# Layer-3 self-attention of a four-layer decoder: bank plan of the spread products, place of the output products, place of the exponential table load

## The chip, the cores and the metric

The kernel runs on one core of one Trainium2 chip (trn2). The metric is the time of one execution on the device in microseconds, as the median over several runs. The kernel before takes 3958.56 us (three runs, 3958.35 to 3964.81).

## What is computed

The program computes twelve sublayers, four layers of self-attention, cross-attention and a feed-forward part, each added to the residual `x` (4 batches x 512 tokens x 256 features, all in float32). The change touches one of them alone, the self-attention of layer 3. It attends over the axis of length 4 (called s for the query and t for the key), separately for each of the 512 tokens and 16 heads of 16 features, with a learned vector for each distance s - t added to keys and values:

```python
Q = (x @ w_q.T).reshape(seq_len, batch, N_HEADS, D_K)   # seq_len = 4, batch = 512
K = (x @ w_k.T).reshape(seq_len, batch, N_HEADS, D_K)
V = (x @ w_v.T).reshape(seq_len, batch, N_HEADS, D_K)
rk = rel_k[rel_idx]
rv = rel_v[rel_idx]
scores = jnp.einsum('sbhd,tbhd->sbth', Q, K) * scale
scores = scores + jnp.einsum('sbhd,std->sbth', Q, rk) * scale
attn = jax.nn.softmax(scores, axis=-1)
out = jnp.einsum('sbth,tbhd->sbhd', attn, V)
out = out + jnp.einsum('sbth,std->sbhd', attn, rv)
out = out.reshape(seq_len, batch, D_MODEL)
return out @ w_o.T + b_o
```

The softmax runs over the last axis, which holds the 16 heads.

## The kernel before

The work of each engine is written out by hand, one instruction stream for each, and ordered by semaphores. Each sublayer is a stage of its own, and all engines meet between stages, so nothing of the next stage starts before the last instruction of this one. The stage is `l3_attn`. It runs in these steps.

1. TensorE (function `unit`, L3900 to L3916) turns the normed tokens and makes queries, keys and values, feature by token, in banks 4 to 7 of PSUM. ScalarE moves each out (`move`, L4007). VectorE multiplies queries with keys for each of the 16 pairs (s, t) (`multiply`, L4068), and TensorE sums them over the heads' features (`scores`, L3922) into banks 0 to 3.
2. Softmax, for t = 0 to 3: ScalarE copies the scores out of PSUM (L4013), TensorE turns them (L3929), VectorE takes maximum and difference (`below_max`, L4104, L4106), ScalarE the exponential (L4016), VectorE sum, reciprocal and share (`share`, L4111 to L4115), TensorE turns the shares back (`turn_shares`, L3935) and ScalarE copies them to `shares_T` (L4019). Ahead of the first exponential the compiler puts an ACT_TABLE_LOAD (L4016).
3. Spread and weigh: `items` lists the 16 pairs as (sp, t, i), with s = 2 sp + i. Two items that differ only in i make a couple. `spread_two` (L3938 to L3953) makes one couple: a product with a constant 32-row matrix copies the 16 shares of a token to its 256 features, two chunks of 128 features for each item, so four products and four banks for a couple. The two items use different 32-row strips. VectorE then makes `(value + rel_v) * spread share` out of PSUM (`weigh`, L4078), 128x1024 for one item, into a ring of eight buffers `weighted_values`. GpSimd (POOL) adds items n and n + 2 of a group of four (L4041), giving eight `attended_pairs_T`.
4. Outputs: `outputs(s)` (L3955 to L3967) multiplies the pairs with `w_o` in 16 products of 128x256, two banks for each s; VectorE adds each half to the residual (`add`, L4083 to L4087).

In steps 3 and 4 the order is given by three things. The spread products use BANKS = 3 slots of two banks, banks 0 to 5, and item n takes slot n % 3. `spread_two` waits, before its first product, until both slots of its couple are free:

```python
for n in (first, first + 1):
    if n >= BANKS:
        pe.wait_ge(weighted, n - BANKS + 1)
    else:
        pe.wait_ge(shares_moved, S)
        pe.wait_ge(unit_moved, len(units))
```

The outputs use banks 6 and 7, whatever s is, and wait for the addition of the s before (`added`). And the streams interleave: TensorE makes `outputs(0)` between couples 5 and 6 (counted from 0), `outputs(1)` between couples 6 and 7, `outputs(2)` and `outputs(3)` at the end; VectorE does the additions of s = 0 after item 13 and those of s = 1 after item 15.

Of the kernel before, what the change touches and what calls it, by code (L numbers as in the profile page):

```python
# [16 lines left out]
ALU = mybir.AluOpType  # L17
ACT = mybir.ActivationFunctionType
AX = mybir.AxisListType

P = 128
D = 256
KC = D // P
B = 4
# [3808 lines left out]
def l3_attn(k):  # L3833
# [10 lines left out]


    nc = k.nc
    S, RING, BANKS = B, 8, 3
    pairs = [(s, t) for n in range(S) for s, t in
             [(m, n) for m in range(n)] + [(n, m) for m in range(n)] + [(n, n)]]
    units = [(kind, s, c) for s in range(S) for kind in ("turn", "query", "key") for c in range(KC)] + [  # L3850
# [2 lines left out]
    ps = k.ps  # L3853
    with ExitStack() as st:
# [3 lines left out]
        head_spread = k.const("head_spread", st)  # L3858
# [12 lines left out]
        e = k.sb("shares_T", [P, S, T], st)  # L3871
        av = k.sb("weighted_values", [P, RING, KC, T], st)
        o = k.sb("attended_pairs_T", [P, 8, KC, T], st)
        items = [(sp, t, i) for sp in range(2) for t in range(S) for i in range(2)]


        def real(w, t):

            return w[:, t, :].rearrange("p (g h) -> p g h", h=32)[:, :, 0:16]

        with signals(nc, "loaded", "stats", "aggr", "shift", "rstd", "normed", "unit_made", "unit_moved",
# [7 lines left out]
            @block.sync  # L3889
            def _(sp):  # L3890
                for w in (wq, wk, wv, rk, rv, head_rows, head_spread, wo, *k.stage_rows):
                    whole = tuple(slice(None) for _ in w.src.shape)
                    sp.dma_start(w.dst[whole], w.src[whole]).then_inc(loaded, 16)
# [4 lines left out]
            def _(pe):  # L3898
# [39 lines left out]
                def spread_two(sp, t):  # L3938
                    first = 8 * sp + 2 * t
                    pe.wait_ge(shares_moved, t + 1)  # L3940
                    for n in (first, first + 1):
                        if n >= BANKS:
                            pe.wait_ge(weighted, n - BANKS + 1)
                        else:
                            pe.wait_ge(shares_moved, S)
                            pe.wait_ge(unit_moved, len(units))
                    for c in range(KC):
                        for i in range(2):
                            r = slice(32 * (2 * sp + i), 32 * (2 * sp + i) + 32)
                            last = pe.matmul(ps[:, 2 * ((first + i) % BANKS) + c, :], head_spread[r, c, :], e[r, t, :],  # L3950
                                             start=True, stop=True)
                            if c == KC - 1:
                                last.then_inc(spread, 1)  # L3953

                def outputs(s):  # L3955
                    sp, i = s // 2, s % 2
                    pe.wait_ge(summed, 4 * sp + 2 + i + 1)
                    for h in range(2):
                        if s:
                            pe.wait_ge(added, 2 * (s - 1) + h + 1)  # L3960
                        for t in (2 * h, 2 * h + 1):
                            for j in range(2):
                                for c in range(KC):
                                    last = pe.matmul(ps[:, 6 + h, t % 2 * D:(t % 2 + 1) * D],
                                                     o[:, 4 * sp + 2 * j + i, c, t * P:(t + 1) * P], wo[:, c, :],
                                                     start=j == 0 and c == 0, stop=j == 1 and c == KC - 1)
                        last.then_inc(made, 1)  # L3967
# [4 lines left out]
                n = 0  # L3972
# [18 lines left out]
                    turn_shares(t)  # L3991
                for sp in range(2):
                    for t in range(S):
                        if sp and t >= 2:
                            outputs(t - 2)
                        spread_two(sp, t)
                outputs(2)
                outputs(3)

            @block.scalar  # L4000
            def _(act):
                dst = {"turn": xT, "query": qT, "key": kT, "value": vT}

                def move(u):
                    kind, s, c = units[u]
                    act.wait_ge(unit_made, u + 1)
                    act.copy(dst[kind][:, s, c, :], ps[:, 4 + u % 4, :]).then_inc(unit_moved, 1)  # L4007

                for u in range(len(units)):
                    move(u)  # L4010
                act.wait_ge(scored, len(pairs))
                for t in range(S):
                    act.copy(sc[:, t, :], ps[:, t, :]).then_inc(scores_moved, 1)  # L4013
                for t in range(S):
                    act.wait_ge(below, t + 1)
                    act.activation(real(er, t), real(er, t), ACT.Exp, scale=0.25).then_inc(exped, 1)  # L4016
                for t in range(S):
                    act.wait_ge(shares_turned, t + 1)
                    act.copy(e[:, t, :], ps[:, t, :]).then_inc(shares_moved, 1)  # L4019
# [25 lines left out]
            def _(dve):  # L4045
# [26 lines left out]
                def weigh(n):  # L4072
                    sp, t, i = items[n]
                    s = 2 * sp + i
                    dve.wait_ge(spread, n + 1)
                    if n >= RING:
                        dve.wait_ge(summed, 2 * ((n - RING) // 4) + i + 1)
                    dve.scalar_tensor_tensor(out=av[:, n % RING, :, :], in0=vT[:, t, :, :],  # L4078
                                             scalar=rv[:, s - t + S - 1:s - t + S],
                                             in1=ps[:, 2 * (n % BANKS):2 * (n % BANKS) + 2, :], op0=ALU.add,  # L4080
                                             op1=ALU.mult).then_inc(weighted, 1)

                def add(s, h):  # L4083
                    dve.wait_ge(made, 2 * s + h + 1)
                    dve.wait_ge(biased, 2 * s + h + 1)
                    rows = k.x[:, TT * s + 2 * h:TT * s + 2 * h + 2, :].rearrange("p t d -> p (t d)")
                    dve.tensor_tensor(rows, rows, ps[:, 6 + h, :], ALU.add).then_inc(added, 1)  # L4087

                batch_stats(0)
                batch_stats(1)  # L4090
# [31 lines left out]
                        share(t - 1)  # L4122
                for n in range(16):
                    weigh(n)
                    if n == 13:
                        add(0, 0)
                        add(0, 1)
                    if n == 15:
                        add(1, 0)
                        add(1, 1)  # L4130
                for s in (2, 3):
                    for h in range(2):
                        add(s, h)
                dve.wait_ge(added, 2 * S)
# [814 lines left out]
```

## Time and profile before

| | |
|---|---|
| median of three runs | 3958.56 us (3958.35 to 3964.81) |
| the profiled execution, its own time | 3928.34 us |
| its span, from first to last instruction | 3926.0 us |
| busy over the whole span: PE, DVE, ACT, POOL | 89%, 56%, 38%, 35% |
| mean granted TensorE clock over the span | 0.931 of full speed |
| stage `l3_attn`, first to last DVE instruction | 2975.59 to 3144.63 us of the span |

A profile is one execution. Its times count from the first instruction. PE is the matmul part of TensorE, PEld its weight loads, DVE is VectorE, ACT ScalarE, POOL GpSimd, SP the engine that issues DMAs. A float32 matmul stands in the profile as two records, so the four products of a couple are eight. In a row of the timeline the first number is the start, the second the length, and the bracket holds how long the engine had been idle and what ended that. A row of busy time by stretch has from and to, the length, the busy time of PE, PEld, DVE, ACT and POOL with the number of instructions of each, the granted clock, and the share and GB/s of DMA. "Granted clock" is the share of TensorE's 2.4 GHz that it was given: 1.00 or, at the lower of the two levels, 0.50 (1.2 GHz).

### The profile page before, as it was taken

Reading aid. Unit: us, or ns where it says so; the run is one execution under the profiler, and the core shown is the slowest. Engines: PE = TensorE matmul, PEld = TensorE weight load, DVE = VectorE, ACT = ScalarE, POOL = GpSimd, SP = SyncE. Lnnn points to the kernel's source line nnn. Section 1 sums busy time; section 2 is a strip of 40 time slices with the busy share of each in tenths; the row PEclk is TensorE's granted clock in tenths of the full one; section 3 lists DMA queues with packets and bytes.
Section 4 is the critical chain, followed back from the end, with each engine's and each line's share of the span. In section 5 each row is a group of like instructions: output and inputs, shape, how many; then the busy total and the mean of one; then the engine's idle time right before and its main releaser. Section 6 shows DMA issues by size and latency. Waiting matters only on the chain. (4 is left out here: it accounts for less than half of the span.)

```text
span 3926.0 us, 54458 instructions
## 1 busy us (share of the span) xinstructions
PE 3483.6 (89%) x18930; PEld 2234.7 (57%) x18930; DVE 2189.6 (56%) x5367; ACT 1495.9 (38%) x3039; POOL 1371.7 (35%) x1904
## 2 busy tenths in 40 slices
PE   7998897899999977789798999998996779996997
PEld 5675684445555567344444555555893445554896
DVE  5374444646556567666366676765334356665454
ACT  2253112434434364233244444443451144442553
POOL 2141441423223245233254444533422144442311
PEclk9999978999999988899799999999898789997998
DMA  2004001000000000000100000001321000003212
GB/s 101 1 1 124 14 1 46 1 1 1 1 1 1 13 1 8 17 1 1 49 1 1 1 1 1 1 1 50 135 76 52 0 29 1 1 1 160 72 60 84
DMA packets 48718, 108.85 MB, mean 28 GB/s; under 512 B 6660, under 2 KB 32900, under 8 KB 46404
## 3 DMA queue, kind: packets, MB, share of 16 engines
q1 hardware_dynamic: 40964, 84.88, 6.4%
q0 software_dynamic: 7488, 20.49, 1.5%
q8 instruction: 158, 2.59, 0.3%
q14 instruction: 108, 0.88, 0.1%
HBM read 70.67 MB, written 34.68 MB: 27 GB/s over the span
## 5 line engine op out<-in xcount | busy, mean ns | idle before, releaser
L2653 POOL TENSOR_SCALAR probs<-probs,inv_sum 128x512 f32<-128x512 f32 x640 | 438.2, 698 | 1007.1 <-DVE inv_sum L2774 1006.8
L2616 ACT ACTIVATE probs<-psum_banks,neg_max 128x576 f32<-128x576 f32 x640 | 468.6, 737 | 743.3 <-DVE neg_max L2857 743.3
L2857 DVE TENSOR_REDUCE neg_max<-psum_banks 128x1 f32<-128x576 f32 x640 | 454.7, 752 | 213.5 <-PE psum_banks L2491 206.9
L2491 PE MATMUL psum_banks<-keys_T,queries_T 64*128 64x288 f32 x2560 | 406.8, 437 | 52.5 <-ACT probs L2616 43.2
L2783 DVE COPY probs_T<-psum_banks 128x512 f32<-128x512 f32 x640 | 408.7, 679 | 4.0 <-PE psum_banks L2411 4.0
L2491 PEld LDWEIGHTS psum_banks<-keys_T,queries_T 64*128 64x128 f32 x2560 | 224.8, 189 | 269.6 <-ACT probs L2616 148.4
L2411 PE MATMUL psum_banks<-ident,probs 128*128 128x128 f32 x2560 | 357.4, 283 | 3.2 <-POOL probs L2653 2.3
L2411 PEld LDWEIGHTS psum_banks<-ident,probs 128*128 128x128 f32 x2560 | 281.2, 143 | 128.9 <-POOL probs L2653 64.8
L2441 PE MATMUL psum_banks<-probs_T,values 128*64 128x512 f32 x1280 | 309.3, 605 | 2.2 <-issue 2.2
L4406 PE MATMUL psum_banks<-sorted_T,tile_weights 128*128 128x128 f32 x2208 | 266.2, 278 | 4.9 <-ACT tile_weights L4496 4.9
L4406 PEld LDWEIGHTS psum_banks<-sorted_T,tile_weights 128*128 128x128 f32 x2208 | 258.5, 195 | 5.7 <-issue 5.6
L2853 DVE TENSOR_TENSOR psum_banks<-psum_banks,key_mask 128x128 f32<-128x128 f32 x192 | 57.4, 299 | 279.9 <-PE psum_banks L2491 279.9
L2665 POOL TENSOR_TENSOR square_sum<-square_sum,neg_half 128x8 f32<-128x8 f32 x102 | 167.1, 1640 | 68.9 <-DVE square_sum L2749 67.6
L4309 POOL DMA_INDIRECT expert_outputs<-expert_rows,output_index x92 | 89.6, 974 | 268.8 <-DVE expert_rows L4683 122.1
L4422 PE MATMUL psum_banks<-w_L_experts_down,hidden_T 128*128 x736 | 177.2, 384 | 7.0 <-DVE expert_rows L4683 3.6
L2346 PE MATMUL psum_banks<-w_L_xattn_Wkv,batch_normed_T 128*128 128x512 f32 x320 | 157.7, 617 | 0.0
L2441 PEld LDWEIGHTS psum_banks<-probs_T,values 128*64 128x64 f32 x1280 | 78.5, 136 | 132.3 <-issue 121.7
L4422 PEld LDWEIGHTS psum_banks<-w_L_experts_down,hidden_T 128*128 128x128 f32 x736 | 134.4, 193 | 23.0 <-issue 8.2
L4496 ACT COPY tile_weights<-w_L_experts_up 128x1024 f32 (+1 forms) x92 | 135.3, 1472 | 25.3 <-issue 25.3
L1962 ACT ACTIVATE probs_T<-psum_banks 128x512 f32<-128x512 f32 (+3 forms) x128 | 83.0, 701 | 127.4 <-PE psum_banks L1899 126.5
L2656 POOL TENSOR_TENSOR context_probs<-probs,inv_sum 128x128 f32<-128x128 f32 x320 | 128.6, 402 | 0.0
L2616 ACT ACTIVATION_READ_ACCUMULATOR probs<-psum_banks,neg_max 128x1 f32 x640 | 125.4, 196 | 0.0
(534 smaller groups left out, 6119.2 us busy)
## 6 DMA issues: line engine op xcount, KB each, us to landing
normed<-sorted_rows SPq DMA_DIRECT2D x30, 385.5 KB, 3.3
sorted_rows<-zero_rows SPq DMA_DIRECT2D x8, 1028.0 KB, 14.6
w_L_experts_down<-in_L_experts_down SPq DMA_DIRECT2D x2, 4096.0 KB, 31.2
normed<-expert_outputs SPq DMA_DIRECT2D x8, 1024.0 KB, 6.9
w_L_xattn_Wkv<-in_L_xattn_Wkv SPq DMA_DIRECT2D x2, 2048.0 KB, 8.1
w_L_experts_up<-in_L_experts_up SPq DMA_DIRECT2D x1, 4096.0 KB, 12.9
sorted_rows<-zero_rows SPq DMA_DIRECT2D x4, 899.5 KB, 14.5
x_res<-in_x SPq DMA_DIRECT2D x4, 512.0 KB, 7.0
```

Of the source, the lines that this page charges most:

```text
L2346: last = pe.matmul(k.ps[:, 7, :], rows, wkv[:, c, W + a * 512:W + (a + 1) * 512], start=c == 0, stop=c == KC - 1)
L2411: last = pe.transpose(k.ps[:, 4 + n % 2, c * P:(c + 1) * P], prob[:, (b * NS + s) % PB, at + c * P:at + (c + 1) * P], k.ident[:, :])
L2441: last = pe.matmul(k.ps[r, 6, :], values[:, b % VB, c, (2 * j + h) * 64:(2 * j + h + 1) * 64], pT[:, q % 2, h, c, :], start=c == 0, stop=F ...
L2491: last = pe.matmul(k.ps[:, 2 * h + a, 0:HALF], qT[r, b % 2, j, t * P:(t + 1) * P], kT[r, j, k0:k0 + HALF], start=True, stop=True)
L2616: act.activation(prob[:, g % PB, h * w:(h + 1) * w].rearrange("p (a n) -> p a n", a=2), k.ps[:, 2 * h:2 * h + 2, 0:HALF], ACT.Exp, bias=nm ...
L2653: pool.tensor_scalar(w, w, inv[:, g % 4, h:h + 1], 1.0, ALU.mult, ALU.mult).then_inc(shared, 1)
L2665: pool.tensor_tensor(ss[:, i % 4, 2, :], ss[:, i % 4, 1, :], k.half[:, 0:8], ALU.pow).then_inc(inverted, 1)
L2783: dve.tensor_copy(pT[:, q % 2, h, :, t * P:(t + 1) * P], k.ps[:, 4 + n % 2, :].rearrange("p (c q) -> p c q", q=P)).then_inc(copied, 1)
L2857: dve.tensor_reduce(nmax[:, g % 4, h:h + 1], k.ps[:, 2 * h:2 * h + 2, 0:HALF], AX.XY, ALU.max, negate=True).then_inc(maxed, 1)
L4406: last = pe.matmul(ps[:, 2 * (n % 2) + part, f * P:(f + 1) * P], wt[:, n % 2, c, part * 512 + f * P:part * 512 + (f + 1) * P], xsT[:, n % ...
L4422: last = pe.matmul(ps[:, 6, 0:D], h[:, n % 2, f * P:(f + 1) * P], w_down[:, f // F, f % F * D:f % F * D + (E - 1) * STEP + D][:, bass.ds(a ...
L4496: act.copy(wt[:, n % 2, :, :], w_up[:, :, 0:(E - 1) * STEP + UP][:, :, bass.ds(at, UP)]).then_inc(weights_copied, 1)
```

## The change

`BANKS` becomes 4, so that the spread products take all eight banks; item n takes slot (n + 2) % 4, so items 0 and 1 begin in banks 4 to 7, which the softmax doesn't use. Only items 2 and 3 wait for all four shares to be moved. All outputs come after all couples, each in the two banks of `item_bank(s)`, and wait for the weighing of the item that last used them instead of for additions; VectorE adds them all after its last item. A one-column exponential (`exp_seed`) stands at the head of ScalarE's stream.

```diff
-    S, RING, BANKS = B, 8, 3
+    S, RING, BANKS = B, 8, 4
...
+        seed = k.sb("exp_seed", [P, 1], st)
         items = [(sp, t, i) for sp in range(2) for t in range(S) for i in range(2)]
 
+
+        def item_bank(n):
+
+            return 2 * ((n + 2) % BANKS)
...
                     for n in (first, first + 1):
                         if n >= BANKS:
                             pe.wait_ge(weighted, n - BANKS + 1)
+                        elif n >= 2:
+                            pe.wait_ge(shares_moved, S)
                         else:
-                            pe.wait_ge(shares_moved, S)
                             pe.wait_ge(unit_moved, len(units))
...
-                            last = pe.matmul(ps[:, 2 * ((first + i) % BANKS) + c, :], head_spread[r, c, :], e[r, t, :],
+                            last = pe.matmul(ps[:, item_bank(first + i) + c, :], head_spread[r, c, :], e[r, t, :],
...
                 def outputs(s):
                     sp, i = s // 2, s % 2
                     pe.wait_ge(summed, 4 * sp + 2 + i + 1)
+                    pe.wait_ge(weighted, len(items) - BANKS + s + 1)
                     for h in range(2):
-                        if s:
-                            pe.wait_ge(added, 2 * (s - 1) + h + 1)
...
-                                    last = pe.matmul(ps[:, 6 + h, t % 2 * D:(t % 2 + 1) * D],
+                                    last = pe.matmul(ps[:, item_bank(s) + h, t % 2 * D:(t % 2 + 1) * D],
...
                 for sp in range(2):
                     for t in range(S):
-                        if sp and t >= 2:
-                            outputs(t - 2)
                         spread_two(sp, t)
-                outputs(2)
-                outputs(3)
+                for s in range(S):
+                    outputs(s)
...
+                act.activation(seed[:, :], k.half[:, 0:1], ACT.Exp)
                 for u in range(len(units)):
                     move(u)
...
                 for n in range(16):
                     weigh(n)
-                    if n == 13:
-                        add(0, 0)
-                        add(0, 1)
-                    if n == 15:
-                        add(1, 0)
-                        add(1, 1)
-                for s in (2, 3):
+                for s in range(S):
                     for h in range(2):
                         add(s, h)
```

TensorE's stream at the end of the stage, before. `head_spread` products are the couples (four for each), `w_o` products the outputs (16 for each s):

```order
L3914 MATMUL psum_banks<-normed_T,w_L_attn_w_v 128x512 x4
L3929 MATMUL psum_banks<-ident,scores_T 128x128 x16
L3935 MATMUL psum_banks<-ident,exps 128x128 x16
L3950 MATMUL psum_banks<-shares_T,w_head_spread 128x512 x24
L3964 MATMUL psum_banks<-w_L_attn_w_o,attended_pairs_T 128x256 x16
L3950 MATMUL psum_banks<-shares_T,w_head_spread 128x512 x4
L3964 MATMUL psum_banks<-w_L_attn_w_o,attended_pairs_T 128x256 x16
L3950 MATMUL psum_banks<-shares_T,w_head_spread 128x512 x4
L3964 MATMUL psum_banks<-w_L_attn_w_o,attended_pairs_T 128x256 x32
```

The same place after the change:

```order
L3927 MATMUL psum_banks<-products,w_head_rows 32x512 x2
L3919 MATMUL psum_banks<-normed_T,w_L_attn_w_v 128x512 x4
L3934 MATMUL psum_banks<-ident,scores_T 128x128 x16
L3940 MATMUL psum_banks<-ident,exps 128x128 x16
L3956 MATMUL psum_banks<-shares_T,w_head_spread 128x512 x32
L3969 MATMUL psum_banks<-w_L_attn_w_o,attended_pairs_T 128x256 x64
```

The number of products is the same, 32 and 64; the 32 products of the outputs of s = 0 and 1 have moved behind the last couple.

ScalarE's stream at the softmax, before:

```order
L4007 COPY values_T<-psum_banks 128x512 x8
L4013 COPY scores_T<-psum_banks 128x512 x4
L4016 ACT_TABLE_LOAD
L4016 ACTIVATE exps<-exps 128x16x16 x4
L4019 COPY shares_T<-psum_banks 128x512 x4
```

ScalarE's stream at the head of the stage, after the change:

```order
L4003 UNCONDITIONAL_BRANCH
L4012 ACT_TABLE_LOAD
L4012 ACTIVATE exp_seed<-neg_half 128x1
L4010 COPY normed_T<-psum_banks 128x512 x2
L4010 COPY queries_T<-psum_banks 128x512 x2
```

The one table load of the stage has moved from between the score copies and the exponentials to the stage's head, with the one-column exponential behind it; no other table load has come or gone in the program.

## Rows read from the trace of the kernel before

**Rows 1.** The page's first line: the span of the profiled execution.

```profile
span 3926.0 us, 54458 instructions
```

**Rows 2.** Timeline of PE from the last turned shares to the stage's end.

```profile
3065.83 2.19 PE L3935 MATMUL psum_banks<-ident,exps 128*128 128x128 f32 x8 [0.75 <-DVE exps L4115]
3068.90 3.78 PE L3950 MATMUL psum_banks<-shares_T,w_head_spread 32*128 32x512 f32 x8 [0.88 <-ACT shares_T L4019]
3074.12 3.78 PE L3950 MATMUL psum_banks<-shares_T,w_head_spread 32*128 32x512 f32 x8 [1.43 <-DVE weighted_values L4078]
...
3094.97 3.78 PE L3950 MATMUL psum_banks<-shares_T,w_head_spread 32*128 32x512 f32 x8 [1.43 <-DVE weighted_values L4078]
3098.68 9.86 PE L3964 MATMUL psum_banks<-w_L_attn_w_o,attended_pairs_T 128*128 128x256 f32 x32
3108.47 1.99 PE L3950 MATMUL psum_banks<-shares_T,w_head_spread 32*128 32x512 f32 x8
3113.70 8.83 PE L3964 MATMUL psum_banks<-w_L_attn_w_o,attended_pairs_T 128*128 128x256 f32 x32 [3.25 <-DVE x_res L4087]
...
3128.25 15.65 PE L3964 MATMUL psum_banks<-w_L_attn_w_o,attended_pairs_T 128*128 128x256 f32 x64 [3.80 <-POOL attended_pairs_T L4041]
```

**Rows 3.** Timeline of DVE: weighing (L4078), additions (L4087), first instruction of the next stage.

```profile
3072.69 2.47 DVE L4078 SCALAR_TENSOR_TENSOR weighted_values<-values_T,w_rel_v_columns,psum_banks 128x1024 f32<-128x1024 f32 x2 [5.83 <-PE psum_banks L3950]
...
3110.49 2.47 DVE L4078 SCALAR_TENSOR_TENSOR weighted_values<-values_T,w_rel_v_columns,psum_banks 128x1024 f32<-128x1024 f32 x2 [9.26 <-PE psum_banks L3950]
...
3143.94 0.69 DVE L4087 TENSOR_TENSOR x_res<-x_res,psum_banks 128x512 f32<-128x512 f32 x1 [2.77 <-PE psum_banks L3964]
3145.67 0.43 DVE L2712 BATCH_NORM_STATS2 batch_stat<-x_res 128x6 f32<-128x256 f32 x1 [1.04 <-PEq L45]
```

**Rows 4.** Busy time and granted clock by stretch of this stage.

```profile
3063.20:3098.70 35.50, 25.95 (x61) 9.76 (x61) 15.80 (x20) 2.64 (x6) 9.30 (x4) 0.50 0.00 0
3098.70:3104.20 5.50, 5.50 (x15) 4.42 (x14) 2.47 (x2) 0.00 (x0) 4.08 (x2) 0.50 0.00 0
...
3128.20:3131.40 3.20, 3.15 (x8) 2.50 (x9) 0.00 (x0) 0.00 (x0) 2.29 (x1) 0.50 0.03 5
3131.50:3144.00 12.50, 12.40 (x58) 10.58 (x56) 2.12 (x4) 0.00 (x0) 0.00 (x0) 1.00 0.00 0
```

**Rows 5.** ACT: its first copy of the stage, and the softmax.

```profile
2981.59 0.59 ACT L4007 COPY normed_T<-psum_banks 128x512 f32<-128x512 f32 x1 [31.73 <-PE psum_banks L3908]
...
3059.14 1.28 ACT L4016 ACT_TABLE_LOAD   x1
...
3068.06 0.59 ACT L4019 COPY shares_T<-psum_banks 128x512 f32<-128x512 f32 x1 [0.49 <-PE psum_banks L3935]
```

**Rows 6.** Timeline of DVE: the stage's first instruction, and the softmax.

```profile
2975.59 1.41 DVE L4049 BATCH_NORM_STATS2 token_stat<-x_res 128x6 f32<-128x256 f32 x4 [1.46 <-PEq L45]
...
3059.72 0.42 DVE L4106 TENSOR_TENSOR exps<-psum_banks,highest 128x256 f32<-128x256 f32 x1
3060.89 0.42 DVE L4111 TENSOR_REDUCE sums<-exps 128x16 f32<-128x256 f32 x1 [0.75 <-ACT exps L4016]
```

**Rows 7.** Instructions on the tile `weighted_values`: ns min/median/max.

```profile
L4078 DVE SCALAR_TENSOR_TENSOR weighted_values<-values_T,w_rel_v_columns,psum_banks x16: 1272/1278/1282, 3072.7 to 3125.7; 128x1024 f32<-128x1024 f32 x16
L4041 POOL TENSOR_TENSOR attended_pairs_T<-weighted_values x8: 2338/2348/2357, 3079.3 to 3128.2; 128x1024 f32<-128x1024 f32 x8
```

**Rows 8.** Busy time and granted clock in the self-attention stage of layer 2.

```profile
1645.00:1655.00 10.00, 8.00 (x82) 3.90 (x84) 6.51 (x11) 3.66 (x7) 3.19 (x10) 1.00 0.01 2
```

**Rows 9.** Groups by line on PE there, 1625 to 1665: a product of 32 rows.

```profile
L1886 PE MATMUL psum_banks<-keys_T,queries_T 32*128 32x512 f32 x16 | 2.3, 640 | 0.0
```

**Rows 10.** Timeline of POOL: the additions of the bias (L4035).

```profile
2988.32 7.45 POOL L4035 TENSOR_TENSOR x_res<-x_res,row_vectors 128x512 f32<-128x512 f32 x6
2996.64 3.47 POOL L4035 TENSOR_TENSOR x_res<-x_res,row_vectors 128x512 f32<-128x512 f32 x2 [0.87 <-DVE normed L4060]
```

**Rows 11.** Timeline of DVE beside the second of these rows.

```profile
2996.48 1.27 DVE L4068 SCALAR_TENSOR_TENSOR products<-keys_T,w_rel_k_columns,queries_T 128x1024 f32<-128x1024 f32 x1
```

More of the change, by code:

```diff
@@ L4079, in weigh @@
                                              scalar=rv[:, s - t + S - 1:s - t + S],
-                                             in1=ps[:, 2 * (n % BANKS):2 * (n % BANKS) + 2, :], op0=ALU.add,
+                                             in1=ps[:, item_bank(n):item_bank(n) + 2, :], op0=ALU.add,
                                              op1=ALU.mult).then_inc(weighted, 1)
@@ L4086, in add @@
                     rows = k.x[:, TT * s + 2 * h:TT * s + 2 * h + 2, :].rearrange("p t d -> p (t d)")
-                    dve.tensor_tensor(rows, rows, ps[:, 6 + h, :], ALU.add).then_inc(added, 1)
+                    dve.tensor_tensor(rows, rows, ps[:, item_bank(s) + h, :], ALU.add).then_inc(added, 1)
                 batch_stats(0)
```

## The prediction

> **What bounds the kernel now.** The chain of waits that ended last covers only the tail of the program, so I read the stage itself: the timeline of PE, then that of DVE beside it, then busy time with the granted clock by stretch. Since all engines meet between stages, whatever this stage saves comes off the program.
>
> In the timeline of PE the reader is to see a rhythm: a couple of spread products takes 3.78 us, then PE stands 1.43 us for a weighing, and the next couple starts 5.22 us after the first [rows 2]. The DVE timeline has the other half: weighing starts 3.79 us after the couple (3068.90 to 3072.69) and takes 2.47 us for two items [rows 2, 3]. Neither engine is full: with three slots a couple needs a slot that the couple before still holds, until its first item is weighed, so the period is 3.79 of PE, one item of 1.28, and the rest a signal, some 0.15. This holds for couples 0 to 5 (3068.90 to 3098.68). After them PE makes the outputs of s = 0 in 9.86 us while DVE idles 9.26 us, couple 6 in 1.99 us, and then waits 3.25 us for the first addition; the same happens again, with couple 7 and another wait of 3.80 us for POOL's sums [rows 2, 3]. The last addition starts at 3143.94 and takes 0.69, the next stage's first instruction follows at 3145.67 [rows 3].
>
> The third view explains the 3.78 against the 1.99: the granted clock is 0.50 through the first six couples, though PE is 73% busy there (25.95 of 35.50), and becomes 1.00 only 5.5 us into the gapless outputs. At 3128.2 outputs begin at 0.50 again and run at 1.00 after 3.2 us [rows 4].
>
> I count from the start of couple 0 (3068.90) to the end of the last addition (3144.63): **75.73 us before**.
>
> **The change, part by part.**
>
> 1. *Four slots.* Couple k now waits for couple k - 2 only. At the low clock PE is the longer one: eight records in two concurrent strips last 3.71 us from one start to the next where no wait lies between (3094.97 to 3098.68 [rows 2]); I estimate 3.4 between two couples, twice the 1.7 that the full clock gives (1.99 less the same tail of 0.3). DVE's 2.47 fits beneath. At the full clock it turns round: PE 1.99, DVE 2.47. A slot pair then needs PE's 2.02 to the first weighing (3108.47 to 3110.49), 2.47 of DVE and 0.15 of signal, 4.64 us for two couples, or 2.32 each, under 2.47: DVE sets the pace [rows 2, 3].
>
> 2. *Which clock.* The trace of before never shows couples without gaps, so I bound it: all eight at the low level, or the rise a few us after the start. Gapless work was granted the full clock after 3.2 us in one row, and after 9.2 us in the other if the couple before the outputs counts (3094.97 to 3104.2) [rows 2, 4]. Now PE has no gap from the turned shares onwards: couple 1 needs no weighing, and couple 2 waits for items 0 and 1, done at 3.79 + 2.47 + 0.15 = 6.4 us, when couple 1 ends (6.8). I take the rise in the middle, about 5 us after the start. Then DVE starts at 3.79 and is not starved again. Does the clock stay up with PE pausing 0.5 us in every 2.47, 80% busy by the profile's measure? Layer 2's self-attention, which has products of 32 rows too, ran at 1.00 with PE busy 8.00 of 10 us [rows 8, 9]. So I say yes.
>
> 3. *The spread phase then.* DVE begins at 3.79; couple 7 waits for six couples weighed: 3.79 + 6 x 2.47 + 0.15 = 18.8. It takes 1.99, so outputs may begin at 20.8. Their new wait, item 12 weighed, ends at 3.79 + 14.8 + 1.28 = 19.9, earlier. Behind that wait on PE's queue lie only the outputs, and their waits on POOL are met early: the sums for s = 0 and 1 are made while DVE weighs, the last one two sums of 2.35 after item 14, at 3.79 + 15 x 1.24 + 4.7 = 27 [rows 7], before outputs of s = 3 want it at 41.5. POOL needs 4.7 for two sums per 4.94 of DVE, so the ring of eight doesn't hold DVE either.
>
> 4. *All outputs at the end.* 64 products, 128 records. At the full clock one half of an s takes the 2.77 idle and 0.69 busy that separate two additions, 3.46 us [rows 3]; eight of them 27.6. Before, the same products took 9.86 + 8.83 + 15.65 = 34.3 [rows 2], partly at the low clock. Additions move behind all weighings on DVE; that costs nothing, since each bank is used once and nobody waits. Only the last shows: some 0.25 for the tail of the last product and 0.69. Sum: 20.8 + 27.6 + 0.9 = **49.3 us**, against 75.7: 26.4 saved.
>
> 5. *An earlier couple 0.* It needs one share moved and banks 4 to 7, not all four shares. Before it stood behind the last copy (3068.06 + 0.59) and began at 3068.90; the turned shares end at 3068.02 [rows 2, 5]. Saved 0.9. Couple 1 waits for all four copies, done 3.4 us before it wants them.
>
> 6. *Table load.* It took 1.28 us between score copies and exponentials, and ended at 3060.42 [rows 5]. DVE waited 0.75 for the exponential between 3059.72 and 3060.89; that goes, then DVE's own chain is next [rows 6]. Saved 0.75 at most; the load now runs from about 2975.6, where ACT has idled and has no work until 2981.59 [rows 5, 6]. A load of 1.28 and a one-column exponential, which I bound by a copy of 512 columns, 0.59, lie in these 6 us. Without that cover they would cost 1.3 to 1.9. I take 0.7.
>
> No DMA or POOL instruction moves, and the next stage begins as before. Together 26.4 + 0.9 + 0.7 = **28.0 us**. The sum is against the profiled execution: 3928.34 would become 3900.3. The median stands 30 us above that execution; its span is 3926.0 [rows 1]. I take the 30 us as common to both kernels, so 3958.56 - 28.0 = **3930.6 us**, 0.7% less.
>
> **Rivals.**
>
> *A. The couples stay at the low clock.* For it: six couples at 73% busy never got the full clock [rows 4]. The Trainium skill has a rule that speaks against this change ("TensorE: Matmul & The Clock Gate", section "A second HAM failure mode: psum-queue depth-cycling"): cycling through PSUM banks, with small pauses between groups of matmuls, made the clock swing between its two levels. By that rule the stage of layer 2 should have swung as well, and it held 1.00 [rows 8]; in this stage the low clock with its pauses agrees [rows 4]. As a mechanism here: couples follow at 3.4, couple 7 begins at 23.9, outputs at 27.6, and their first 5.5 us are at half speed, 2.7 lost: 27.6 + 27.6 + 2.7 + 0.9 = 58.8, saved 16.9 + 1.6 = 18.5, **3940 us**. Against it: the pauses of 1.43 are gone [rows 2].
>
> *B. POOL and DVE block each other.* DVE now weighs without pause while POOL sums. Such a block exists: six bias additions took 1.24 each, but two beside a DVE product took 3.47 [rows 10, 11]. The Trainium skill ("SBUF — State Buffer", "Who interferes with whom") gives the case: a DVE instruction with two inputs in SBUF against a GpSimd one that reads SBUF. By it the weighing, with one array in SBUF and one in PSUM, is free of it. The rows say the same: the sums took 2338 to 2357 ns, whether a weighing lay beside them, as at 3079.3, or not [rows 7]. If all ran in series, item 12 would be weighed at 3.79 + 13 x 1.24 + 6 x 2.35 = 34.0 and outputs would begin there, not at 20.8: 13.2 less saved, **3944 us**.
>
> *C. Slower: the sums become the bound.* Same place, larger price. All outputs of s = 2 and 3 wait for a chain of eight sums that begins 7.5 us in. With x us for each, the end is 7.5 + 8x + 6.9 + 0.9. That reaches the 77.3 of before (75.7 + 1.6) at x = 7.8, and at 9 it is 10 us slower, **3968 us**. The sum measures 2.35 in all eight cases [rows 7], so x would have to grow more than threefold. Nothing in the trace hints at it.
>
> *D. The change doesn't do it:* another wait keeps the 5.2 us rhythm. The stream shows none. Gain then only from outputs and start, some 5 us, **3953**.
>
> **How the numbers follow.** Forecast 0.75, A 0.18, B 0.03, C 0.02, D 0.02. A measurement of this kernel can tell about 0.2%, 8 us, from no change; forecast, A and B lie beyond it: faster 0.96, D is same 0.02, C slower 0.02. The range: the clock's rise anywhere from 3 to 9 us moves the forecast by 1 to 2, other moments of rising and falling in the 780 us behind the stage by some 4 (the runs of before spread over 6.5). That gives 3924 to 3937 for the forecast alone, and A asks for 3943 above. I give 3922 to 3943.
>
> **What would show it.** In the profile after: couple starts 3.4 us apart at first, then 2.5; DVE's weighings in one row with at most one or two waits of a us; granted clock 1.00 within 10 us of couple 0 and kept; additions 3.46 apart; the last addition some 49 us behind couple 0; no wait of PE on additions. Part 6 is right if the first sum of exponentials starts 0.7 us earlier relative to the score copies. A shows as 0.50 up to the outputs, B as sums longer than 2.4 or weighings over 1.3. The forecast is wrong if PE waits between couples for POOL, or if the stages behind take longer than before.

## The result and the profile after

| | before | after | ratio |
|---|---|---|---|
| median, first measurement (10 runs each) | 3958.93 us | 3943.07 us (3936.77 to 3951.31) | 0.9959, interval 0.9951 to 0.9967 |
| median, second chip | 3932.26 us | 3916.00 us | 0.9950, 0.9937 to 0.9962 |
| median, third measurement | 3958.28 us | 3944.71 us | 0.9964, 0.9950 to 0.9977 |
| profiled execution, own time | 3928.34 us | 3942.55 us | |
| its span | 3926.0 us | 3940.4 us | |

The change is faster by 15.9 us, 0.4%, where I forecast 28.0; the third measurement has 13.6. The two profiled executions may not be set against each other as wholes: the nine stages ahead of the changed one have the same code, yet took 2970 us in the one and 2994 in the other, above all the feed-forward stage of layer 2 (241.7 and 262.8 us). That stage took 260.3 us in a later profile of the kernel before with one idle instruction, on another chip. So I compare stages.

The timeline of PE after, from the last turned shares to the stage's end; it answers to [rows 2]:

```profile
3089.10 2.19 PE L3940 MATMUL psum_banks<-ident,exps 128*128 128x128 f32 x8 [0.75 <-DVE exps L4119]
3091.22 27.29 PE L3956 MATMUL psum_banks<-shares_T,w_head_spread 32*128 32x512 f32 x64
3118.44 29.21 PE L3969 MATMUL psum_banks<-w_L_attn_w_o,attended_pairs_T 128*128 128x256 f32 x128
```

The waits of 1.43 us are gone: all eight couples are one row without a gap, and all outputs another. But 27.29 us for eight couples are 3.41 each, which is the low clock's pace. The timeline of DVE, answering to [rows 3]:

```profile
3095.04 2.47 DVE L4082 SCALAR_TENSOR_TENSOR weighted_values<-values_T,w_rel_v_columns,psum_banks 128x1024 f32<-128x1024 f32 x2 [4.92 <-PE psum_banks L3956]
3098.45 2.47 DVE L4082 SCALAR_TENSOR_TENSOR weighted_values<-values_T,w_rel_v_columns,psum_banks 128x1024 f32<-128x1024 f32 x2 [0.94 <-PE psum_banks L3956]
...
3118.51 2.47 DVE L4082 SCALAR_TENSOR_TENSOR weighted_values<-values_T,w_rel_v_columns,psum_banks 128x1024 f32<-128x1024 f32 x2 [0.94 <-PE psum_banks L3956]
3123.51 0.69 DVE L4091 TENSOR_TENSOR x_res<-x_res,psum_banks 128x512 f32<-128x512 f32 x1 [2.52 <-PE psum_banks L3969]
...
3147.68 0.69 DVE L4091 TENSOR_TENSOR x_res<-x_res,psum_banks 128x512 f32<-128x512 f32 x1 [2.77 <-PE psum_banks L3969]
3149.41 1.40 DVE L2712 BATCH_NORM_STATS2 batch_stat<-x_res 128x6 f32<-128x256 f32 x4 [1.04 <-PEq L45]
```

DVE waits 0.94 us for PE in nearly every couple: PE still sets the pace, not DVE. Busy time and granted clock by stretch, answering to [rows 4]:

```profile
3091.20:3118.40 27.20, 27.20 (x65) 10.59 (x64) 17.31 (x14) 0.59 (x1) 13.98 (x6) 0.50 0.00 1
3118.40:3120.90 2.50, 2.50 (x8) 2.01 (x7) 2.39 (x2) 0.00 (x0) 1.03 (x1) 0.50 0.00 0
3121.20:3148.40 27.20, 26.45 (x123) 22.94 (x121) 5.50 (x8) 0.00 (x0) 3.34 (x2) 1.00 0.00 1
```

PE was busy for 27.20 of 27.20 us and was granted 0.50 all along; 2.5 us of outputs later it had 1.00. From couple 0 to the end of the last addition it is 57.15 us (3091.22 to 3148.37), against 75.73 before and 49.3 forecast. From the first DVE instruction of this stage to that of the next it is 149.43 us against 170.07 before (168.95 and 149.15 in the second pair of profiles, below).

ScalarE's head of the stage, answering to [rows 5], and the start of its softmax:

```profile
2999.95 1.28 ACT L4012 ACT_TABLE_LOAD   x1 [25.65 <-PEq L45]
3001.24 0.20 ACT L4012 ACTIVATE exp_seed<-neg_half 128x1 f32<-128x1 f32 x1
3005.99 0.59 ACT L4010 COPY normed_T<-psum_banks 128x512 f32<-128x512 f32 x1 [4.54 <-PE psum_banks L3913]
...
3081.16 2.06 ACT L4017 COPY scores_T<-psum_banks 128x512 f32<-128x512 f32 x4
3083.49 0.42 ACT L4020 ACTIVATE exps<-exps 128x256 f32<-128x256 f32 x1 [0.26 <-DVE exps L4110]
```

Load and seed end 4.5 us before the first copy wants ScalarE. The sums of POOL are as short as before, 2338 to 2359 ns, with DVE weighing almost without pause beside them:

```profile
L4045 POOL TENSOR_TENSOR attended_pairs_T<-weighted_values x8: 2338/2352/2359, 3099.8 to 3122.2; 128x1024 f32<-128x1024 f32 x8
```

Two questions were left. Why did gapless couples not get the full clock? And why do the medians differ by 15.9 us when the stage is 20.6 us shorter?

### The profile page after: what moved, and what is told of

The parts are those of the page before. It is cut to its first block and busy times, and to the rows that moved or that the text cites. A ratio compares the mean times of both kernels' runs of the same rounds, so it can differ in the third digit from the quotient of the medians.

```text
span 3940.4 us, 54458 instructions
## 1 busy us (share of the span) xinstructions
PE 3495.3 (89%) x18930; PEld 2240.6 (57%) x18930; DVE 2191.8 (56%) x5367; ACT 1495.8 (38%) x3040; POOL 1370.0 (35%) x1904
## 5 line engine op out<-in xcount | busy, mean ns | idle before, releaser
L2441 PE MATMUL psum_banks<-probs_T,values 128*64 128x512 f32 x1280 | 310.9, 607 | 2.2 <-issue 2.2
L2853 DVE TENSOR_TENSOR psum_banks<-psum_banks,key_mask 128x128 f32<-128x128 f32 x192 | 57.5, 299 | 280.1 <-PE psum_banks L2491 280.1
L2441 PEld LDWEIGHTS psum_banks<-probs_T,values 128*64 128x64 f32 x1280 | 78.8, 136 | 133.8 <-issue 124.1
```

The lines of the kernel that those rows point to most:

```text
L2441: last = pe.matmul(k.ps[r, 6, :], values[:, b % VB, c, (2 * j + h) * 64:(2 * j + h + 1) * 64], pT[:, q % 2, h, c, :], start=c == 0, stop=F ...
```

## Experiments on the clock

All are edits of the changed kernel unless said. "The 57.15" is its time from couple 0 to the end of the last addition.

### Products over all 128 rows

```diff
-    r = slice(32 * (2 * sp + i), 32 * (2 * sp + i) + 32)
-    last = pe.matmul(ps[:, item_bank(first + i) + c, :], head_spread[r, c, :], e[r, t, :],
+    last = pe.matmul(ps[:, item_bank(first + i) + c, :], wide.dst[:, 2 * sp + i, c, :], e[:, t, :],
                      start=True, stop=True)
```

> The changed kernel, but each spread product uses all 128 rows (a constant with zeros outside its strip), so the products of a couple no longer run two at a time. Theory 1 (two 32-row strips don't bring the full clock, products of 128 rows do): at 0.50 a couple takes 6.8 us, the clock becomes 1.00 some 3 to 9 us after couple 0, then couples follow every 3.4 us; couple 0 to the end of the last addition about 59 us. Theory 2 (the cycling through banks keeps the clock low, whatever the rows): 0.50 throughout, couples 6.8 us apart, 85 to 88 us.

The timeline of PE, and below it the stretches (same columns as [rows 4]):

```profile
3078.15 29.16 PE L3957 MATMUL psum_banks<-shares_T,w_head_spread_wide 128*128 128x512 f32 x64
3107.16 27.79 PE L3970 MATMUL psum_banks<-w_L_attn_w_o,attended_pairs_T 128*128 128x256 f32 x128
```

```profile
3074.40:3081.10 6.70, 5.89 (x16) 3.53 (x17) 2.62 (x8) 2.55 (x5) 0.00 (x0) 0.50 0.00 0
3081.40:3107.10 25.70, 25.70 (x61) 11.40 (x60) 17.92 (x15) 0.00 (x0) 14.05 (x6) 1.00 0.00 1
```

The clock was at 1.00 by 3.3 us after couple 0 and stayed there. The products no longer ran two at a time, so each couple took twice the cycles, at twice the clock: 29.0 us for eight, and 57.5 in all against 57.15. The banks, their order, the waits and the gaplessness are those of the change. So theory 1 holds against the rival that cycling through banks keeps the clock low, whatever the rows. But two things differ from the change at once: a product has 128 rows where it had 32, and products run one at a time where they ran two. No run tells these apart, so "32-row strips" stands below for both together.

The Trainium skill, which I had weighed in the prediction ("TensorE: Matmul & The Clock Gate", section "A second HAM failure mode: psum-queue depth-cycling"), tells of cycling through banks together with small pauses between groups of matmuls. Here neither the change (27.20 of 27.20 us busy, 0.50) nor this run (25.70 of 25.70, 1.00) had such pauses, so the low clock of the change is no case of it, and this run is no test of it.

### Couple 0 begins at the full clock

Four products of 128x512 whose results nobody reads fill PE's pauses in the softmax:

```diff
+    pe.wait_ge(unit_moved, len(units))
     for t in range(S):
+        for n in range((2, 1, 1, 0)[t]):
+            pe.matmul(ps[:, 4 + (t + n) % 4, :], wq[:, 0, 0:P], xT[:, 0, 0, :], start=True, stop=True)
         turn_shares(t)
```

> The changed kernel with four idle products of 128x512 between the turned scores and the turned shares (results unused), so that couple 0 begins at the full clock. Theory 1a (two strips can't raise the clock but can hold it): 1.00 through all couples, DVE's 2.47 us sets the pace, couple 0 to the end of the last addition 47.5 us, 9.7 us less than the change's 57.15. Theory 1b (two strips can't hold it either): it falls to 0.50 within 3 to 7 us of couple 0 and stays there until the outputs, 53 to 56 us.

The timeline of PE from couple 0, and below it the stretches:

```profile
3074.94 3.70 PE L3956 MATMUL psum_banks<-shares_T,w_head_spread 32*128 32x512 f32 x16
3079.57 19.40 PE L3956 MATMUL psum_banks<-shares_T,w_head_spread 32*128 32x512 f32 x48 [0.94 <-DVE weighted_values L4085]
```

```profile
3074.90:3080.40 5.50, 4.56 (x21) 2.00 (x22) 3.44 (x3) 0.58 (x1) 0.00 (x0) 1.00 0.00 0
3080.60:3100.80 20.20, 20.20 (x51) 8.35 (x48) 15.40 (x14) 0.00 (x0) 14.46 (x7) 0.51 0.00 1
3101.10:3128.80 27.70, 26.93 (x124) 23.31 (x123) 5.85 (x9) 0.00 (x0) 3.90 (x2) 0.99 0.00 1
```

In these stretches couple 0 starts at 1.00, and 6 us later the clock is at 0.50 until the outputs. From couple 0 to the end 53.8 us (3074.94 to 3128.76): theory 1b. Two strips did not bring the full clock in the change, and did not hold it here. The evidence for the fall is weaker: at 1.00 PE outran DVE and paused once, 0.94 us, ahead of couple 2, and the clock fell 1.4 us after that pause. That two strips would lose the clock without any pause is not shown. What is shown is that they did not get it back: 20.2 us without a gap stayed at 0.50.

### The same with a small product of 128 rows ahead of each couple

```diff
+    pe.matmul(ps[:, item_bank(first), 0:D], wq[:, 0, 0:P], xT[:, 0, 0, 0:D], start=True, stop=True)
     for c in range(KC):
```

This stands in the function that issues a couple's spread products, and comes on top of the edit above.

> keep_warm, and ahead of each couple one more idle product of 128 rows and 256 columns into the bank that the couple then overwrites (0.43 us at the full clock). Theory 1 (what counts is how much 128-row work lies in a stretch, so a mixture can hold the clock that two strips alone lose): 1.00 from couple 0 to the last output, couples 2.5 us apart, couple 0 to the end of the last addition 48 to 49.5 us against the change's 57.15, and in the median some 8 us less than the change. Rival (any stretch of two-strip products lets it fall): 0.50 within 7 us of couple 0, couples 4.3 us apart from there, 56 to 60 us.

Stretches, then the last rows of PE's timeline, then DVE's first two:

```profile
3066.30:3087.00 20.70, 20.38 (x82) 7.74 (x80) 17.27 (x14) 0.58 (x1) 13.11 (x6) 1.00 0.00 1
3087.00:3115.60 28.60, 27.91 (x130) 24.24 (x128) 7.98 (x11) 0.00 (x0) 5.58 (x3) 1.00 0.00 1
```

```profile
3084.50 0.67 PE L3953 MATMUL psum_banks<-normed_T,w_L_attn_w_q 128*128 128x256 f32 x2
3085.10 1.99 PE L3957 MATMUL psum_banks<-shares_T,w_head_spread 32*128 32x512 f32 x8
3087.01 27.89 PE L3970 MATMUL psum_banks<-w_L_attn_w_o,attended_pairs_T 128*128 128x256 f32 x128
```

```profile
3068.86 5.02 DVE L4086 SCALAR_TENSOR_TENSOR weighted_values<-values_T,w_rel_v_columns,psum_banks 128x1024 f32<-128x1024 f32 x4 [3.09 <-PE psum_banks L3957]
3074.09 5.02 DVE L4086 SCALAR_TENSOR_TENSOR weighted_values<-values_T,w_rel_v_columns,psum_banks 128x1024 f32<-128x1024 f32 x4 [0.22 <-PE psum_banks L3957]
```

Clock 1.00 throughout, couples 2.6 us apart, DVE idle 0.22 us in four items and PE busy for 20.38 of 20.70 us, couple 0 to the end 48.8 us (3066.84 to 3115.63). This is the course that I had forecast for the change, at 49.3. The filling products also take up PE's pauses (none is over 0.2 us), so the run does not tell the 128 rows of the filling from the missing pause. Twelve products that compute nothing take 8.5 us off the stage (149.15 to 140.68, profiles of one chip). Medians 3903.12 us against 3916.00 of the change and 3932.26 before, on one chip; ratio to before 0.9929 (0.9916 to 0.9942). Once more, beside the change on a slower chip:

> warm_and_filled once more beside the changed kernel, on one chip. The stages behind and ahead left out, 8.5 us lie between them in the profiles (149.2 and 140.7 us for the stage), and 3.6 more in the cross-attention behind (444.0 and 440.5). So 12 us between the medians if both hold, ratio to the kernel before 0.992; 8 us if the cross-attention's part is chance.

> The changed kernel beside it: ratio to the kernel before 0.995 to 0.996, its stage 148 to 150 us, the cross-attention behind it 444 us again.

3930.76 us against 3944.71 and 3958.28; ratios to before 0.9937 (0.9922 to 0.9951) and 0.9964 (0.9950 to 0.9977). The stage took 141.1 and 149.3 us, the cross-attention behind it 440.9 and 444.1. The medians are 13.95 us apart, 12 expected. So this version beats both kernels, the one before by 27.5 to 29 us.

### The small product without the start at the full clock

> The change with the idle product ahead of each couple, but without the idle products in the softmax, so couple 0 begins at 0.50. If the mixture is enough to hold the full clock but not to bring it: 0.50 up to the outputs, couples 4.3 us apart, 63 to 66 us from couple 0 to the end of the last addition. If it also brings it: 1.00 within 9 us of couple 0, then couples 2.5 us apart, 51 to 53 us.

The edit is the last one alone. The stretch of its couples:

```profile
3078.30:3117.00 38.70, 38.70 (x81) 13.30 (x80) 17.30 (x14) 0.59 (x1) 13.98 (x6) 0.50 0.00 0
```

0.50 up to the outputs, without a gap: the mixture held the full clock and did not bring it. My size was off: couples came 4.87 us apart, not 4.3, and it took 68.9 us from couple 0. A product of 128 rows and a couple do not overlap as two couples do: the small product began 3.71 us behind its couple, as in [rows 2], against 3.41 between couples, and the next couple 1.15 us behind the small product, where I had allowed 0.86.

## Experiments on the parts

### Three slots, outputs still at the end

```diff
-    S, RING, BANKS = B, 8, 4
+    S, RING, BANKS = B, 8, 3
...
-            return 2 * ((n + 2) % BANKS)
+            return 2 * (n % BANKS)
+
+        def out_bank(s):
+
+            return (6, 2, 4, 0)[s]
```

> The changed kernel with three slots for the spread products instead of four (outputs still all at the end, early table load kept). If the fourth slot brings most: couples 5.2 us apart, outputs from 40 us behind couple 0, 71 us to the end of the last addition against the change's 57.15 and 75.73 before. If the outputs' place brings most: under 64 us.

```profile
3071.10:3111.30 40.20, 30.19 (x65) 10.08 (x65) 17.31 (x14) 0.00 (x0) 13.95 (x6) 0.50 0.00 0
```

Couple 0 waits for all four shares again here, as before; the count begins behind that wait. This stretch is the eight couples: PE busy 30.19 of 40.20, couples 5.21 us apart, 70.1 us to the end. Of the 18.6 us between 75.73 and 57.15, the outputs' place brought 5.6 and the fourth slot 13.0.

### The table load back in the softmax

```diff
-                act.activation(seed[:, :], k.half[:, 0:1], ACT.Exp)
```

> The changed kernel without the early exponential, so the table load is back in the softmax. If the load lay on the path, the first sum of exponentials is 0.7 us later behind the first score copy and the stage is 0.7 us longer than the change's 148.8 us. If it was hidden, no difference over 0.1 us.

```profile
3065.85 2.06 ACT L4016 COPY scores_T<-psum_banks 128x512 f32<-128x512 f32 x4
3067.93 1.28 ACT L4019 ACT_TABLE_LOAD   x1
```

```profile
3069.67 0.42 DVE L4114 TENSOR_REDUCE sums<-exps 128x16 f32<-128x256 f32 x1 [0.74 <-ACT exps L4019]
```

The first sum comes 3.82 us behind the first score copy, against 3.00 with the change (3081.16 to 3084.16), and couple 0 is 0.84 us later behind that copy. The stage is 1.4 us longer, not 0.7. Besides the 0.84, the outputs take 1.03 us more (30.24 against 29.21), because the clock rose 4.8 us into them here and 2.7 with the change, and the score copies came 0.47 us sooner in the stage. The moment of the rise differs from run to run: it came 2.5 and 2.6 us into the outputs in the two other profiles of the change, and 5.5 in late_by_two (below), which has the same instructions up to there.

## Experiments on the 4 us that were given back

The two stages behind the changed one have the same instructions in all kernels. The lengths of the changed stage and of the first of them, from the first DVE instruction of a stage to that of the next:

```text
                     this stage   cross-attention of layer 3 behind it
before                 170.07        439.91
before_again           168.95        439.86
after                  149.43        444.11
after_again            149.15        444.05
after_third            149.25        444.08
```

> The kernel before once more, for a second profile. If the 4 to 5 us between what the stage gains in the profiles (20.65 us) and what the medians differ (15.9 us) lie in this stage's clock, its length differs by some us from the 169.5 us of the first profile; if they lie in other stages, the stage agrees within 1 us and the others differ by more.

> The changed kernel once more. Its stage: 148.8 us in the first profile; if the moment at which the clock rises within the outputs is left to chance, 147.5 to 151. Its gain over the kernel before, on another chip: 13 to 19 us if it holds there as measured, 20 if the first measurement was low by chance.

The stage gained 20.2 us on average (169.5 to 149.3; 20.6 and 19.8 in the two pairs), and the cross-attention took 4.2 us more each time. The difference, 16.0 us, is near what the medians show: 15.9 and 16.3, and 13.6 in the third measurement. The last stage, the feed-forward of layer 3, is not in the table. It took 340.4 us before and 346.9 after in the first pair, but 340.0 in both of the second. In all profiles of chips 2 and 8 it took 339.4 to 340.5, in all four of chip 4 347.7 to 348.2, whatever the kernel. So the 6.5 us most likely go with the chip and not with the change; which chips the first pair ran on is not on record.

The cross-attention behind and its granted clock, before and after:

```profile
3145.70:3585.60 439.90, 383.20 (x1928) 212.19 (x1928) 286.22 (x637) 178.53 (x394) 189.59 (x260) 0.95 0.02 7
```

```profile
3149.40:3593.50 444.10, 386.86 (x1928) 213.50 (x1928) 286.38 (x636) 178.55 (x394) 189.41 (x260) 0.94 0.02 7
```

The same 1928 matmul records cost PE 3.7 us more, and its weight loads 1.3; the busy times of DVE, ACT and POOL moved by less than 0.2. One place near its end, in PE's timeline of before and of after:

```profile
3562.55 1.32 PE L2411 MATMUL psum_banks<-ident,probs 128*128 128x128 f32 x8 [2.29 <-POOL probs L2653]
...
3565.43 3.65 PE L2441 MATMUL psum_banks<-probs_T,values 128*64 128x512 f32 x16 [0.72 <-issue]
```

```profile
3568.07 1.82 PE L2411 MATMUL psum_banks<-ident,probs 128*128 128x128 f32 x8 [2.29 <-POOL probs L2653]
...
3571.72 5.32 PE L2441 MATMUL psum_banks<-probs_T,values 128*64 128x512 f32 x16 [0.72 <-issue]
```

The sixteen records of L2441 take 3.65 us in the one and 5.32 in the other: the clock fell ahead of them after the change, and did not before. To see whether this hangs on when the stage begins, I tried to move only that. In the kernel before, by one idle addition on DVE at the end of the stage (0.42 us and its waits):

```diff
                 dve.wait_ge(added, 2 * S)
+                dve.tensor_tensor(qk[:, 2, 0, 0:D], qk[:, 2, 0, 0:D], qk[:, 1, 0, 0:D], ALU.add).then_inc(delayed, 1)
+                dve.wait_ge(delayed, 1)
```

> The kernel before, with one idle addition of 128x256 on DVE behind the stage's last one, about 0.45 us. If the cross-attention's length hangs on its starting moment against the clock's changes, this moves it to where the changed kernel starts it: 444 us instead of 439.9. If it comes from what the change leaves behind: 439.9 as before.

and in the changed kernel by two larger ones, 1.22 and 0.69 us with their waits:

> The change, with two idle additions on DVE behind the stage's last one, about 2.15 us, so that the next stage begins that much later. The cross-attention of layer 3 behind it has the same instructions in all kernels, yet took 439.9 us in both profiles before and 444.1 in both after (440.5 in three experiments). If that hangs on when it begins relative to the moments at which the clock changes: 440 to 441 us here, so that the two stages together get some 1.4 us shorter though the first is 2.15 longer. If it comes from what the change leaves behind (banks, tables, semaphores): 444 as with the change.

```profile
3164.60:3606.90 442.30, 384.92 (x1928) 213.03 (x1928) 286.43 (x637) 178.49 (x394) 189.59 (x260) 0.94 0.02 7
```

```profile
3146.20:3588.40 442.20, 384.40 (x1928) 213.18 (x1928) 286.39 (x637) 178.44 (x394) 189.62 (x260) 0.94 0.02 7
```

The first row is the kernel before with its addition: 442.3 us, 2.4 more than without. The second is the changed kernel with its two: 442.2, 1.9 less than without. Neither value is the one expected. But the kernel before has nothing of the change in it, and its cross-attention left 439.9 all the same; the rival, something that the change leaves behind, predicted 439.9 and 444 and does not explain this.

The idle additions were not the only thing that moved. They put the next stage off by 0.47 and 2.00 us behind the last addition. By chance the clock also rose later in the outputs ahead of them, 6.2 us into the last ones and not 3.2 in the kernel before, 5.5 and not 2.7 in the changed one. The moment of the rise can be read from a stretch of 1 us in which it falls: 0.94 means that it came 0.12 us after the start of the stretch. Here are after, late_by_two, no_seed, before and before_late:

```profile
3121.00:3122.00 1.00, 1.00 (x5) 0.83 (x5) 0.00 (x0) 0.00 (x0) 1.00 (x1) 0.94 0.00 0
3117.00:3118.00 1.00, 1.00 (x5) 0.83 (x5) 0.00 (x0) 0.00 (x0) 0.91 (x1) 0.85 0.00 0
3108.00:3109.00 1.00, 1.00 (x4) 0.83 (x3) 0.00 (x0) 0.00 (x0) 1.00 (x1) 0.63 0.00 0
3131.00:3132.00 1.00, 1.00 (x5) 0.85 (x4) 0.00 (x0) 0.00 (x0) 0.00 (x0) 0.77 0.00 0
3151.00:3152.00 1.00, 1.00 (x5) 0.85 (x4) 0.00 (x0) 0.00 (x0) 0.00 (x0) 0.78 0.00 0
```

From such rows, the time between the clock's last rise and the first DVE instruction of the cross-attention, beside that stage's length:

| | rise to the stage behind | cross-attention |
|---|---|---|
| after, after_again, after_third, keep_warm, three_slots | 28.3 to 28.4 us | 444.0 to 444.1 us |
| late_by_two | 28.9 | 442.2 |
| filled_only, no_seed | 27.0, 27.2 | 440.5 |
| before, before_again | 14.2, 14.4 | 439.9 |
| before_late | 13.2 | 442.3 |

Five profiles of three kernels agree in the one number within 0.1 us and in the other as well, and a shift of 1 us in the one goes with as much as 3.6 us in the other. (In wide_rows the clock rose 55.5 us ahead, 444.2; in the two profiles with the full clock throughout 129.5 and 129.1 us ahead, 440.5 and 440.9.) That is what one would see if the stage behind hung on when it begins as measured by the clock's rises, whichever kernel is ahead of it. It is read off these profiles and not tested: no run set that time. Waiting paid nothing: late_by_two has 2.75 us more in the first stage, 2.00 of them its additions, for 1.9 less in the second.

## Why the prediction was off, step by step

The direction was right and so was the account of what bounds the stage before. The size was forecast at 28.0 us and is 15.9; the median, 3943.07, lies at the upper end of the range, 7 hundredths of a us beyond it. That it lies so near is luck: the forecast alone asked for 3924 to 3937, the upper end was set for rival A, whose own time was 3940, and two things that neither had in its sum worked against each other: the gain in the stage was 1.7 us larger than A's, and 4.2 us were lost in the stage behind.

- **Four slots (step 1)**: right. No wait of PE between couples, and 3.41 us from couple to couple at the low clock, 3.4 estimated.
- **Which clock (step 2)**: this step failed. I let the clock rise 5 us after couple 0. It never rose before the outputs, whatever the gaps, and rival A describes the course: outputs 27.2 us behind couple 0 (27.6 worked out there, 20.8 in the forecast). The error lay in what I took for the cause of the low clock in [rows 4]: the gaps of 1.43 us. The other difference from the work that had risen was there to see in [rows 2], 32 rows against 128. The stage that I called as witness in [rows 8, 9] mixes products of 32 rows with those of 128 (13.9 us of the 33.3 that PE was busy from 1625 to 1665); warm_and_filled shows that a mixture can hold the clock where two strips alone didn't. Nor did that stage hold 1.00, as I wrote against rival A: [rows 8] is 10 us of it, and it was granted 0.77 from 1600 to 1620 and 0.91 from 1700 to 1720. The step cost 6.4 us in the couples.
- **The spread phase (step 3)**: 2.47 us from couple to couple, set by DVE, was never seen over the whole phase. In keep_warm PE waited 0.94 us for a weighing ahead of couple 2, then the clock fell; in warm_and_filled couples came 2.6 apart, with PE and DVE both nearly full. POOL and the ring held nobody, as said.
- **Outputs at the end (step 4)**: right at the full clock, additions 3.45 us apart; but the first 2.7 us of outputs ran at 0.50 and cost 1.4 us. With the 6.4 that makes the 7.8 us between 49.3 and 57.15. Rival A charged 2.7 for this and was too dear by 1.3.
- **Earlier couple 0 (step 5)**: 0.9 us forecast. Behind the first score copy couple 0 comes 11.84 us before, 10.90 without the early table load, 10.06 with the change: 0.94.
- **Table load (step 6)**: 0.84 us, 0.7 forecast.
- **What lies behind**: I gave the stages behind some 4 us of either sign as chance. In the profiles it was not that: all three of the change lost 4.2 us in the cross-attention. 28.0 less 7.8 is 20.2, which is what the stage gained on average, and 20.2 less 4.2 is 16.0.
- **Rivals B, C and D**: sums of 2338 to 2359 ns and weighings of 1275 to 1281 rule out B and C. D is ruled out by the PE timeline.

## What to carry to other kernels

Before a sum counts on the full clock, look for a row of the same kind of product at that clock, not for gapless work in general; here 128-row work had it and work on two 32-row strips, just as gapless, had not. An engine that seems full can be full at half its clock, and a few products that compute nothing can gain more than they cost: twelve of them took 8.5 us off this stage. And compare stage by stage: the first stage's length and that of unchanged ones behind it tell a gain that was given back from one that never came.

## What the runs showed of the hardware

- Gapless products on two 32-row strips stayed at 0.50 for 27.2 us (the change). Begun at 1.00 they were at 0.50 after 6 us, with one pause of 0.94 us in them (keep_warm). 128-row products in the same places came to 1.00 by 3.3 us (wide_rows). With one 128-row product of 256 columns for each couple, 1.00 was held for 20.7 us (warm_and_filled) but not reached from 0.50 in 38.7 us (filled_only). 32-row products one at a time, and four strips at once without 128-row work between, were not tried.
- Couples on two strips at once at 0.50 and 128-row products one behind the other, nearly all at 1.00, cost about the same, 27.2 and 29.0 us for eight couples (the latter with 3 us at the low level).
- A stage of 440 us with unchanged instructions varied between 439.9 and 444.2 us, and profiles of one kernel agreed within 0.1 us in two kernels (before, after) and within 0.4 in a third (warm_and_filled). Equal times from the clock's last rise to its beginning went with equal lengths. Differences below 0.1% of this kernel say nothing about an edit unless the stages behind are looked at.
